# A ninth split step per item, with three places for the high and low parts of the weights

## What is computed

```
h = token_mixer(x)                      # rFFT amplitudes, two attention layers, windowed sums -> (8, 344, 64)
h = h + retention(layernorm(h))
h = h + product_key_attention(layernorm(h))
```

```
index  = idx0[:, None] + 64 * idx1[None, :]        # 16 of 4096 by score
k = einsum('bnhk,bnhkd->bnhd', softmax(scores), keys_table[ind])
v = einsum('bnhk,bnhkd->bnhd', softmax(scores), values_table[ind])
out = softmax(causal(q @ k.T)) @ v                 # per head
out = out @ Wo
```

## Time and profile before

| what | value |
|---|---|
| median of 3 runs | 1929.27 us |
| lowest, highest | 1928.9, 1929.72 us |
| profiled execution | 1929.85 us |
| its span, first to last instruction | 1928.1 us |
| mean granted TensorE clock | 0.99 |
| TensorE matmul busy, share of span | 1861.4 us, 97% |
| VectorE | 1608.8 us, 83% |
| ScalarE | 1460.5 us, 76% |
| GpSimd | 1318.5 us, 68% |

### The profile page before, as it was taken

How to read it: one execution, slowest core, us unless ns; L and a number is a source line. 1 busy time by engine, 2 the same in 40 slices (tenths; PEclk the granted TensorE clock), 3 DMA queues, 4 the chain that set the end, 5 groups by cost and what they waited for, 6 DMA issues and landing times.

```text
span 1928.1 us, 43717 instructions
## 1 busy us (share of the span) xinstructions
PE 1861.4 (97%) x11464; PEld 1402.9 (73%) x11464; DVE 1608.8 (83%) x4824; ACT 1460.5 (76%) x2969; POOL 1318.5 (68%) x1576
## 2 busy tenths in 40 slices
PE   5997899999999999999999999999999999999997
PEld 3765577777777777777777777777777777777775
DVE  3646788888888888888888888888888888888886
ACT  3763477878778778878877778877887777878785
POOL 1211477777777777777777777777777777777775
PEclk9998899999999999999999999999999999999998
DMA  3001110002000200011000200020001100020001
GB/s 109 2 1 48 58 22 20 17 16 63 21 20 20 62 17 18 20 41 44 19 15 17 64 20 20 19 61 16 20 20 26 60 15 16 19 65 20 20 18 28
DMA packets 118622, 58.00 MB, mean 30 GB/s; under 512 B 110224, under 2 KB 116560, under 8 KB 117261
## 3 DMA queue, kind: packets, MB, share of 16 engines
q1 hardware_dynamic: 115778, 56.75, 11.6%
q10 hardware_dynamic: 2795, 0.70, 0.2%
HBM read 24.55 MB, written 0.70 MB: 13 GB/s over the span
## 4 chain that ended last, share of the span: by engine, by line
POOL 42%; issue 38%; PE 7%; POOLq 2%; DVE 1%; SPq 0%; ACT 0%; DMA 0%; DVEq 0%; ACTq 0%
POOL k_W_low L1399 25%; POOL k_aS L1341 3%; POOL k_cand L1355 2%; POOL k_ecs L1385 2%; POOL k_tab_low L1404 2%; PE ps L980 2%; POOL k_aS L1348 2%; PE ps L971 1%; PE ps L988 1%; POOL k_aS L1346 1%; POOLq L1398 1%; POOL k_small L1370 1%; POOL k_ecs L1366 1%; POOL k_small L1371 1%; POOL k_off L1375 1%
## 5 line engine op out<-in xcount | busy, mean ns | idle before, releaser
L1399 POOL TENSOR_TENSOR k_W_low<-k_W,k_W_high 128x688 fp32r<-128x688 f32 x513 | 851.5, 1660 | 320.0 <-ACT k_W_high L1213 316.8
L1208 ACT ACTIVATE k_W<-ps 128x688 f32<-128x688 f32 x1029 | 770.4, 749 | 338.0 <-PE ps L971 325.7
L1565 DVE SCALAR_TENSOR_TENSOR k_W<-ps,k_W 128x688 f32<-128x688 f32 x1028 | 889.1, 868 | 162.0 <-ACT k_W L1208 148.5
L980 PE MATMUL ps<-k_W,k_tab 128*128 128x344 f32 x2048 | 676.6, 453 | 0.0
L971 PE MATMUL ps<-k_X,sel 128*128 128x344 f16 x2058 | 472.4, 311 | 17.9 <-DMA k_X<-k_spl 9.5
L980 PEld LDWEIGHTS ps<-k_W,k_tab 128*128 128x128 f32 x2048 | 366.3, 190 | 127.0 <-issue 0.5
L1213 ACT ACTIVATE k_W_high<-k_W 128x688 fp32r<-128x688 f32 x513 | 398.4, 777 | 0.8
L988 PE MATMUL ps<-k_W_high,k_tab_high 128*128 128x344 f32 x1024 | 385.9, 379 | 0.0
L971 PEld LDWEIGHTS ps<-k_X,sel 128*128 128x128 f16 x2058 | 164.7, 98 | 238.3 <-issue 77.6
L988 PE MATMUL ps<-k_W_high,k_tab_low 128*128 128x344 f32 x1024 | 323.6, 319 | 0.0
L992 PE MATMUL ps<-k_W_low,k_tab_high 128*128 128x344 f32 x1024 | 246.6, 322 | 0.0
(11 more groups left out here) (234 smaller groups left out, 2301.8 us busy)
## 6 DMA issues: line engine op xcount, KB each, us to landing
k_tab<-in_tables SPq DMA_DIRECT2D x9, 2048.0 KB, 7.2
k_X<-k_spl SPq DMA_TRANSPOSE x390, 2.4
k_xs<-x2T SPq DMA_DIRECT2D x66, 86.0 KB, 2.0
k_qT<-k_qs SPq DMA_DIRECT2D x33, 86.0 KB, 2.0
cst<-in_consts SPq DMA_DIRECT2D x1, 1024.0 KB, 20.4
wts<-in_weights SPq DMA_DIRECT2D x1, 896.0 KB, 13.0
cst<-in_consts SPq DMA_DIRECT2D x1, 874.5 KB, 17.9
xr<-in_xrows SPq DMA_DIRECT2D x1, 750.0 KB
```

The source lines that it names most:

```text
L980: mm = mm_(sums, tab[:, slot, at + k, :], W[:, d % RING, k, :], start=(d == 0 and k == 0), stop=(d == NDC - 1 and k == 1))
L1208: A(W[:, d % RING, :, :], ps[:, 2 * (d % 2):2 * (d % 2) + 2, 0:LOUT], ACT.Exp).then_inc(e_done, 1)
L1399: G.tensor_tensor(W_low[:, q % SPLIT_RING, :, :], W[:, d % RING, :, :], W_high[:, q % SPLIT_RING, :, :].bitcast(F32), ALU.subtract).then_i ...
L1565: V.scalar_tensor_tensor(W[:, d % RING, :, :], ps[:, 2 * (d % 2):2 * (d % 2) + 2, 0:LOUT], 0.0, W[:, d % RING, :, :], ALU.is_ge, ALU.mult) ...
```

## The change

`SPLITS` becomes a list of nine steps: the eight odd ones and step 14. So an item has seven plain and nine split steps, with 13, 14 and 15 in a row. The rows of the tables that have two parts are now those of d % 4 in (1, 2, 3), 24 blocks instead of 16, and each piece of them made in an item has three blocks instead of two (`NPART` 3, 384 elements wide). Steps 2, 6 and 10 have such rows as well but stay plain. The rings of `W_high` and `W_low` have three places instead of four; the place is worked out by `part_slot`. The attention output on TensorE moves from behind step 13 to behind step 14, and `add_output` on VectorE from pass 14 to pass 15.

```diff
-        SPLIT = (1, 3)
-        SPLITS = [d for d in range(NDC) if d % 4 in SPLIT]
+        SPLIT = (1, 2, 3)
+        SPLITS = [1, 3, 5, 7, 9, 11, 13, 14, 15]
         NSPLIT = len(SPLITS)
-        NPART = 2 * NSPLIT // 8
-        FIRST_ROW = (2, 6)
-        RING, SPLIT_RING = 8, 4
+        NPART = len(SPLIT)
+        FIRST_ROW = (2, 5)
+        RING, SPLIT_RING = 8, 3
...
-        tab_high = sb("tab_high", [128, 2, 2 * NSPLIT, 128], F32R)
-        tab_low = sb("tab_low", [128, 2, 2 * NSPLIT, 128], F32R)
+        tab_high = sb("tab_high", [128, 2, 8 * NPART, 128], F32R)
+        tab_low = sb("tab_low", [128, 2, 8 * NPART, 128], F32R)
...
+        def part_slot(d, par):
+
+            return (split_at(d) + NSPLIT * par) % SPLIT_RING
+
...
-                                mm_(sums, t[:, slot, at + k, :], W_high[:, q % SPLIT_RING, k, :],
+                                mm_(sums, t[:, slot, at + k, :], W_high[:, part_slot(d, par), k, :],
...
-                            if d == 13:
+                            if d == 14:
                                 attention_output(i)
...
-                    A(W_high[:, split_at(d) % SPLIT_RING, :, :], W[:, d % RING, :, :], ACT.Copy).then_inc(high_done, 1)
+                    A(W_high[:, part_slot(d, par), :, :], W[:, d % RING, :, :], ACT.Copy).then_inc(high_done, 1)
...
                                 largest_score(i + 2)
+                            if d == 15:
                                 add_output(i, pair * 2 if par else ((pair + 3) % 4) * 2 + 1)
```

More of the change, by code:

```diff
@@ L991, in table_sum @@
                         for k in range(2):
-                            mm = mm_(sums, tab_high[:, slot, at + k, :], W_low[:, q % SPLIT_RING, k, :], start=False,
+                            mm = mm_(sums, tab_high[:, slot, at + k, :], W_low[:, part_slot(d, par), k, :], start=False,
                                      stop=(d == NDC - 1 and k == 1))
@@ L1208, in exponentials, with weights_high @@
                     A(W[:, d % RING, :, :], ps[:, 2 * (d % 2):2 * (d % 2) + 2, 0:LOUT], ACT.Exp).then_inc(e_done, 1)
-                def weights_high(i, d):
+                def weights_high(i, d, par):
                     act.wait_ge(main_done, i * NDC + (split_before(d, SPLIT_RING) + 1 + ahead(main_done)))
                     act.wait_ge(w_done, i * NDC + (d + 1))
-                    A(W_high[:, split_at(d) % SPLIT_RING, :, :], W[:, d % RING, :, :], ACT.Copy).then_inc(high_done, 1)
+                    A(W_high[:, part_slot(d, par), :, :], W[:, d % RING, :, :], ACT.Copy).then_inc(high_done, 1)
                 def table_high(slot, loads, pair, half):
@@ L1273, in _ @@
                     if d in SPLITS:
-                        weights_high(0, d)
+                        weights_high(0, d, 0)
                 class Body:
@@ L1292, in item @@
                                 if d + LEAD - 2 < NDC:
-                                    weights_high(i, d + LEAD - 2)
+                                    weights_high(i, d + LEAD - 2, par)
                                 else:
-                                    weights_high(i + 1, d + LEAD - 2 - NDC)
+                                    weights_high(i + 1, d + LEAD - 2 - NDC, 1 - par)
                             if d == 2:
@@ L1394, in low_part, with weights_low @@
                                     spl[:, :, :, 0, :], ALU.subtract).then_inc(low_step, 1)
-                def weights_low(i, d):
+                def weights_low(i, d, par):
                     q = split_at(d)
                     pool.wait_ge(high_done, i * NSPLIT + (q + 1))
-                    G.tensor_tensor(W_low[:, q % SPLIT_RING, :, :], W[:, d % RING, :, :], W_high[:, q % SPLIT_RING, :, :].bitcast(F32),
+                    G.tensor_tensor(W_low[:, part_slot(d, par), :, :], W[:, d % RING, :, :], W_high[:, part_slot(d, par), :, :].bitcast(F32),
                                     ALU.subtract).then_inc(low_done, 1)
@@ L1423, in _ @@
                     if d in SPLITS:
-                        weights_low(0, d)
+                        weights_low(0, d, 0)
                 class Body:
@@ L1448, in item @@
                                 if d + LEAD - 2 < NDC:
-                                    weights_low(i, d + LEAD - 2)
+                                    weights_low(i, d + LEAD - 2, par)
                                 else:
-                                    weights_low(i + 1, d + LEAD - 2 - NDC)
+                                    weights_low(i + 1, d + LEAD - 2 - NDC, 1 - par)
                             if d == 7:
```

## The result

The changed kernel takes 1935.28 us in the median of 14 runs (1930.14 to 1936.47), the old one 1929.56 us in the 14 runs beside it (1927.07 to 1931.32). The ratio is 1.0026, with a 95% interval from 1.0019 to 1.0034: slower by 5.0 us, 3.7 to 6.6, by that ratio (the two medians lie 5.7 us apart). The profiled execution took 1932.92 us, its span is 1931.1 us against 1928.1, so it shows 3.0 us of it.

A forecast was written before the change was run, and what follows sets the result against it. TensorE was taken to set the pace. Its gain of 14.1 us from step 14 and a new wait of 15.8 us summed to +1.7 us on the median 1929.27: 1931.0 us, range 1921 to 1938.

The forecast's parts named there:

- the two large terms: TensorE's saving from splitting step 14, -14.1 us, and its new wait in front of that step, +15.8 us.
- The gain of step 14: TensorE's step 14, once split, takes 1.23 instead of 1.45 us: 0.22 us per item, 14.1 us over 64 items.
- ScalarE's insertion and the wait behind it: W_high(14) and a longer table copy before exponential W(17), 1.13 us, make TensorE wait before step 14: 15.8 us over 62 items.
- the chain of five links: From exponential W(16) through W_high(14), table copy, exponential W(17) and mask to TensorE's step 14: 3.47 us.
- the two kinds: Items alternate between two kinds, differing in ScalarE's backlog; waits before step 14 of 0.33 us in the first, 0.18 in the second.
- GpSimd: W_low(14), 1.62 us, and a larger table part hide in idle time; W_low(1) of the next item has 0.7 us to spare.
- the rival of 2007 us: VectorE's copy of turned probabilities is held by GpSimd's W_low(14), so TensorE starts step 14 1.23 us later: 76 us, chance 3%.
- add_output moved: nothing: Moving add_output from VectorE's pass 14 to 15 costs nothing, as its reader, the spreading of gains, is over 2 us later.
- two items that don't repeat the two kinds: Exceptions counted among the 64 items: the first and one at which a table is loaded; the wait was summed over 62.
- the prediction's own sign: It called itself wrong if waits in steps 0 to 11 change at all, which would point to GpSimd becoming late.
- the third rival: GpSimd becomes the late engine and TensorE waits in step 1 or 11: 0.2 us per item, 13 us, 1944 us; chance 5%.
- The ring of three places: W_high and W_low copies wait for a step three split steps back, already met by the exponential ahead: nothing.

The follow-up runs named there:

- the last two versions with nine splits: Changed kernel, attention output and add_output back in old places, turned-probability copies ahead of W_high(15): 1918.33 us; the same with ScalarE's table part in pass 6: 1917.87 us.
- The first experiment: Changed kernel with ScalarE's table part made early, in pass 6 instead of pass 11: 1921.65 us, ratio 0.9959 to the kernel before.

## Why the prediction was right

The direction and the mechanism were right, and so were the sizes of the two large terms: 1931.0 us was forecast, 1935.28 measured, inside the range of 1921 to 1938. The net change is another matter, +1.7 forecast and 5.0 measured: it is the small difference of two large terms, and a third term was missing. Slower had 27% and no change within 0.2% had 53%; the measured 0.26% lies just above that border.

- *The gain of step 14.* Step 14 goes from 1.45 to 1.24 us instead of 1.23; 0.21 us, 13.4 us in all. Step 15 gets 0.02 us longer, which the forecast left out. In the last two versions with nine splits, where the wait is gone, the items are 0.2 and 0.17 us shorter and the time falls by 11 us, not by 14.
- *ScalarE's insertion and the wait behind it.* 0.33 and 0.18 us forecast, 0.31 and 0.15 measured in the two items shown; the chain of five links was 0.02 us too long. The items of the two kinds change by +0.08 and -0.03 us, where +0.11 and -0.04 were worked out. The first experiment showed that the wait hangs on ScalarE's queue, by taking one piece out of it. The waits for the mask grew by 18.8 us in all; the 15.8 of this term and the 1.6 of the loop's ends are 17.4 of it.
- *GpSimd.* Forecast W_low(1) with 0.7 us to spare, the rows give about 0.7 (1022.59 against 1022.41 + 0.92). Not late. The copy of the turned probabilities was not held: the row at 1015.66 has the same 0.37 us as before, while W_low(13) runs and W_low(14) is about to. The prediction reads the page that it names as giving the other case, and that reading is wrong. In the Trainium skill (SBUF — State Buffer, Who interferes with whom) a copy takes the port pair only when its operands allow the modes that use both ports, and outside those modes a VectorE instruction with at most one input in SBUF does not contend with GpSimd. This copy reads PSUM and has no input in SBUF. The trace agrees, with its 0.37 us, so that page does not give the rival of 2007 us.
- *add_output moved: nothing.* This term was wrong. Its reader is indeed 2 us away, but at the three returns of the outer loop VectorE's sequencer reaches the branch only when the last instruction of the body is handed over, and that sets when the engine is back at its first mask. It costs 0.5 to 0.6 us each time, 1.6 us in the profile of the change. The rows of before had the place: the prediction counts two items that don't repeat the two kinds, but there are five, and the three it missed (27.52, 27.62 and 27.49 us, where others of their kind have 25.73) hold the long step 0. By the prediction's own sign, a changed wait in the steps 0 to 11, this is where it was wrong, but not by the third rival's cause. The move alone measured +2.3 us (0.6 to 4.1), and undoing it in the version with the early table part came with -3.8 us, 1.7 of it at these steps.
- *The rest.* +1.7 forecast (1.5 measured over the items) and 1.6 for the loop's ends give 3.3 us, near the 3.0 us of the two spans. The repeated runs say 5.0 (3.7 to 6.6). Their profile was not taken, so where the other 2 us lie stays open; single long steps next to the loop's ends (a step of 1.94 us and one of 2.09 us behind the first end in the old kernel with the move, one of 2.62 us behind the third end in the version with the early table part) are a candidate, not shown for the change itself.
- *The ring of three places* was held to cost nothing. It was not tried by itself. ScalarE idles 0.8 us in all in front of the 577 copies of the changed kernel, in the page's row above, and 0.8 us in front of the 513 before, so no wait for a place shows.

## What to carry to other kernels

A shorter step on the bound engine is worth only what the chain that feeds it can follow. Before shortening, lay the feeding engines' rows beside it. The same ninth split cost 5 us with the attention output moved, cost 23 us with it in its old place, and gained 11 us in that old place once two copies stood ahead of another on ScalarE. The difference was which instruction of 0.4 to 0.7 us stood ahead of the one that was waited for. Moving a piece of work that covered a wait moves the cover too, so count both ends of the move. And in a tenth step the same recipe failed on an engine that was 87% busy, through two operations of 0.24 us behind long ones.

## What the runs showed of the hardware that was not expected

At the three returns of the outer loop VectorE's sequencer takes 2.7 to 3.1 us from the branch to its next instruction, in all nine traces. At the returns of the inner loop it is 0.3 us at most. ScalarE, whose loop has four more copies to `W_high` per body in the changed kernel, shows the same for the first time there:

```profile
655.45 0.74 ACT L1212 ACTIVATE k_W<-ps 128x688 f32<-128x688 f32 x1 [2.62 <-issue]
```

In the old kernel the exponential at that place was at 653.17, waiting for TensorE, and ScalarE's sequencer went on 0.2 us after its branch; with the change it takes 2.5 to 2.7 us. GpSimd's takes 0.2 in both. TensorE waited for the mask, so VectorE's gap was the later one.

What happens in the gap shows in the DMA queues. From the branch to the next instruction, 651.6 to 654.5 before and 652.4 to 655.3 after, the queue for instructions moves one packet of 8 KB before and two after (packets, MB, share):

```profile
q14 instruction: 1, 0.01, 1.1%
```

```profile
q14 instruction: 2, 0.02, 1.8%
```

At this return the packets start 1.0 to 1.1 us after VectorE's branch and take 0.3 to 0.5 us. Over one whole round of the outer loop the queue moves 5 such packets before and 10 after. So the gap holds a fetch of instructions. That one packet is VectorE's and the second ScalarE's is an inference from the counts; the packets don't carry the engine's name. What makes ScalarE fetch again in the changed kernel is not shown either. Its loop body became longer: it executes 1565 recorded instructions per round instead of 1501 (VectorE 1773 in both, GpSimd 781 instead of 749). No run varied the length by itself.

For a kernel this means that such a return costs an engine some 3 us from its branch on, and that the branch comes when the last instruction of the body is handed over. Work that makes this instruction late costs there, 0.5 to 0.6 us three times here.
